# An adaLN feed-forward kernel on one core: K sums, a load of the down weights and three small steps are moved in the order of work

## The reference

```python
K = 2.0 * jnp.einsum('hn,hnl->hl', Cs, jnp.exp(P)).real     # 32 heads, n = 64, l = 512
y = causal_convolution(u * mask, K) + (u * mask) * D[:, None]
y = y * mask
```

```python
xq    = int4_quant(y)                          # beta = mean |y| of the row
gate  = bitlinear(xq, w_gate);  up = bitlinear(xq, w_up)      # 512 -> 1376
inter = int8_quant(up * square(relu(gate)))    # gamma = max |.| of the row
out   = x + bitlinear(inter, w_down)           # 1376 -> 512
```

## Time and profile before

| | |
|---|---|
| median of three runs | 205.91 us |
| the profiled execution's own time | 205.13 us |
| its span | 203.0 us |
| outside the span | 2.13 us |
| TensorE busy | 174.0 us (86%) |
| VectorE busy | 166.2 us (82%) |
| ScalarE (ACT) busy | 114.2 us (56%) |
| mean granted TensorE clock | 0.992 |

### The profile page before, as it was taken

The page is one execution under the profiler, slowest core; times in us unless marked ns, Lnnn a source line. Parts: engine busy times, 40 slices in busy tenths (PEclk is TensorE's granted clock), DMA queues, the critical chain, the costliest instruction groups (busy, mean ns, idle before and its releaser), DMA issues.

```text
span 203.0 us, 3423 instructions
## 1 busy us (share of the span) xinstructions
PE 174.0 (86%) x1127; PEld 93.7 (46%) x1143; DVE 166.2 (82%) x456; ACT 114.2 (56%) x188; POOL 11.7 (6%) x31
## 2 busy tenths in 40 slices
PE   1001699899899999999999999999999999998883
PEld 1001696554545454545454545454544454443352
DVE  6999888779997698888888878787878797978871
ACT  2186986799717282819191918182727364644730
POOL 8122500100001000000000000000000000000000
PEclk9999969999999999999999999999999999999999
DMA  2999939376898376756666665659565687245504
GB/s 84 371 385 338 316 103 332 124 247 124 164 187 174 138 152 204 151 164 143 176 133 185 134 182 135 184 129 183 132 182 149 157 137 181 67 96 56 116 6 103
DMA packets 48224, 34.12 MB, mean 168 GB/s; under 512 B 36512, under 2 KB 36880, under 8 KB 48208
## 3 DMA queue, kind: packets, MB, share of 16 engines
q1 hardware_dynamic: 47408, 32.38, 64.1%
q10 hardware_dynamic: 416, 1.47, 2.0%
q0 software_dynamic: 384, 0.06, 0.3%
HBM read 21.07 MB, written 4.28 MB: 125 GB/s over the span
## 4 chain that ended last, share of the span: by engine, by line
PE 70%; DVE 12%; DMA 7%; ACT 7%; issue 3%; SPq 0%; DVEq 0%; ACTq 0%
PE conv_ps L508 16%; PE gate_ps L591 15%; PE down_ps L641 15%; PE up_ps L596 14%; PE tr_act_ps L498 3%; DMA q_int<-y_i 2%; DMA toep<-k_back 2%; DMA k_back<-k_sb 2%; ACT g L749 1%; ACT int_gate L692 1%; ACT int_down L685 1%; DVE inter L1107 1%; PE tr_dve_ps L641 1%; PE up_ps L544 1%; PE tr_dve_ps L565 1%
## 5 line engine op out<-in xcount | busy, mean ns | idle before, releaser
L596 PE MATMUL up_ps<-up_t,q_t 128*128 128x416 bf16 (+2 forms) x192 | 45.0, 357 | 0.0
L707 ACT ACTIVATE y_abs<-y 128x512 bf16<-128x512 f32 x16 | 10.1, 629 | 61.1 <-DVE y L1022 61.1
L591 PE MATMUL gate_ps<-gate_t,q_t 128*128 128x416 bf16 (+2 forms) x177 | 41.9, 356 | 2.4 <-DVE q_t L1042 1.5
L1107 DVE SCALAR_TENSOR_TENSOR inter<-up_ps,gu_scale,g 128x416 f32<-128x416 f32 (+2 forms) x48 | 33.2, 692 | 6.8 <-issue 4.6
L508 PE MATMUL conv_ps<-toep,x_t 128*64 128x512 f32 (+3 forms) x256 | 38.0, 439 | 0.7 <-DMA toep<-k_back 0.5
L641 PE MATMUL down_ps<-down_t,i_t 128*128 128x512 bf16 (+1 forms) x153 | 35.3, 379 | 1.2 <-DVE i_t L1146 1.2
L749 ACT ACTIVATE g<-gate_ps,gu_scale 128x416 f32<-128x416 f32 (+2 forms) x48 | 30.3, 631 | 6.1 <-PE gate_ps L591 6.1
L1111 DVE TENSOR_REDUCE imax<-inter 128x1 f32<-128x416 f32 (+2 forms) x48 | 30.3, 631 | 1.6
L752 ACT ACTIVATE g<-g 128x416 f32<-128x416 f32 (+2 forms) x48 | 28.1, 585 | 1.5
L508 PEld LDWEIGHTS conv_ps<-toep,x_t 128*64 128x64 f32 x256 | 17.2, 136 | 23.5 <-issue 20.5
L596 PEld LDWEIGHTS up_ps<-up_t,q_t 128*128 128x128 bf16 x192 | 18.8, 98 | 18.4
(11 more groups left out here) (186 smaller groups left out, 170.9 us busy)
## 6 DMA issues: line engine op xcount, KB each, us to landing
toep<-k_back SPq DMA_DIRECT2D x16, 512.0 KB, 4.0
out_dram<-o_sb SPq DMA_DIRECT2D x30, 128.0 KB, 2.4
x_in<-in_x_dram SPq DMA_DIRECT2D x24, 128.0 KB, 3.1
raw_gate<-in_L_ffn_w_gate_dram SPq DMA_DIRECT2D x1, 1536.0 KB, 7.0
raw_up<-in_L_ffn_w_up_dram SPq DMA_DIRECT2D x1, 1536.0 KB, 13.5
raw_down<-in_L_ffn_w_down_dram ACTq DMA_DIRECT2D x1, 1376.0 KB, 6.9
raw_down<-in_L_ffn_w_down_dram SPq DMA_DIRECT2D x1, 1376.0 KB, 10.8
raw_gate<-in_L_ffn_w_gate_dram SPq DMA_DIRECT2D x1, 1024.0 KB, 9.3
```

The lines of the kernel that those rows point to most:

```text
L591: mm = pe.matmul(gate_ps[bank][:, 0:cn], q_t[p][:, i, :], gate_t[:, i, c0:c0 + cn], start=(i == 0), stop=(i == KB - 1))
L596: mm = pe.matmul(up_ps[bank][:, 0:cn], q_t[p][:, i, :], up_t[:, i, c0:c0 + cn], start=(i == 0), stop=(i == KB - 1))
L1107: v.scalar_tensor_tensor(out=inter[:, c0:c0 + cn], in0=up_ps[bank][:, 0:cn], scalar=gu_scale[p][:, 1:2], in1=g2[bank][:, 0:cn], op0=ALU.mu ...
```

## The change

Four things are moved; no arithmetic is changed.

1. SP no longer loads x of tile 1 in front of the zeros of `k_back`. After the Toeplitz tile of tile 0 it now loads x of tile 1, then half 0 of w_down, then the Toeplitz tile of tile 1, then half 1. The load of half 0 on ACT's queue is gone.
2. `k_sums(3)` leaves iteration 1. Its first four heads are multiplied in the prologue behind `k_sums(1)`, its last four behind `qt(0)`. `xt(0)` is put ahead of `mean(1)`.
3. On VectorE `q_copy(0)` is put ahead of `k_copy(2)`, and `q_copy(2)` ahead of the cast to i_t and of `gated(2)` in iteration 1.
4. On ACT `xt_copy(3)` is put ahead of `relu_square(2)` in iteration 1.

```diff
@@ sync
             load_x(0)
-            load_x(1)
...
+            def load_down(i):
+                s = weight_part(2, i)
+                sp.dma_start(raw[2][s], w_down.rearrange("(c p) i -> p c i", p=P)[s]).then_inc(w_loaded[2][i], 16)
+
             load_toep(0, 0)
+            load_x(1)
+            load_down(0)
             load_toep(1, 1)
-            s = weight_part(2, 1)
-            sp.dma_start(raw[2][s], w_down.rearrange("(c p) i -> p c i", p=P)[s]).then_inc(w_loaded[2][1], 16)
+            load_down(1)
             load_x(2)
@@ tensor
+        K_CUT = 3 * HG // 4
...
-            def k_sums(i):
+            def k_sums(i, first=0, last=HG):
...
-                for h in range(h0, h1):
+                for h in range(max(h0, first), min(h1, last)):
...
-                mm.then_inc(k_summed, 1)
+                if last >= h1:
+                    mm.then_inc(k_summed, 1)

             k_sums(0)
+            xt(0, 0, 0)
             mean(1)
-            xt(0, 0, 0)
             pe.wait_ge(tables_ready, 2)
             k_sums(1)
+            pe.wait_ge(winv_ready, 2)
+            k_sums(3, last=K_CUT)
             turn_inner(0, 0, range(3, IG))
...
             k_sums(2)
             qt(0)
+            k_sums(3, first=K_CUT)
...
-                if k == 1:
-                    k_sums(3)
@@ scalar
-            s = weight_part(2, 0)
-            act.dma_start(raw[2][s], w_down.rearrange("(c p) i -> p c i", p=P)[s]).then_inc(w_loaded[2][0], 16)
...
                 if k == 1:
                     y_round(2)
+                    xt_copy(3)
...
-                elif k < T - 2:
+                elif 2 <= k < T - 2:
                     xt_copy(m + 2)
@@ vector
             weight_copy(10)
+            q_copy(0, 0)
             k_copy(2)
-            q_copy(0, 0)
             down_sum(2)
...
                 if k in (1, T - 1):
                     gated(1)
+                if k == 1:
+                    q_copy(2, 0)
...
-                if 1 <= k < T - 1:
+                if 2 <= k < T - 1:
                     q_copy(m + 1, 1 - p)
```

## The result

| | median us | lowest to highest | runs |
|---|---|---|---|
| before | 206.11 | 205.87 to 206.24 | 5 |
| changed | 209.28 | 208.88 to 210.14 | 5 |

The ratio is 1.0152, with a 95% interval of 1.0117 to 1.0186: the change made the kernel slower, by 3.2 us. Here and in the experiments medians are of all runs, while ratios and their intervals leave out runs over 1.5% above the fastest of the same kernel (211.60 and 209.94 of e3, 208.15 of the kernel before). The profiled execution took 210.14, with a span of 208.2; it is the slowest of the five, and the kernel before was profiled in an execution of 205.13, under all five of its runs. So the rows show the loss larger (5.2 us by the spans, 208.2 against 203.0) than the medians do.

A forecast was written before the change was run, and what follows sets the result against it. Iterations run at TensorE's pace, so lateness before 60 us carries to the end; +2.4 - 0.2 - 0.7 + 1.3 = +2.8 on the profiled 205.13 gives 207.9, as a median 208.7; range 205.6 to 211.6.

The forecast's parts named there:

- A: The forecast case: stall at down_sum(0), two or three us net; 208.7 us, from 207.2 to 210.0; chance 0.55.
- Store and Toeplitz issue: Prologue: store of K's part 0 takes 2.2 us instead of 3.60; Toeplitz load issued at 26.1, 1.4 us gained.
- Landing of half 0: Prologue: half 0 of w_down lands at 34.9, so down_sum(0) starts then instead of at 32.49: +2.4 us.
- (b): Landing estimate for half 0 by parts: Toeplitz as measured, x and weights at 400 GB/s: 34.3.
- (c): Landing estimate for half 0 from half 1's measured load, stragglers included: 36.6.
- K sums: Prologue: half ahead of weight transposes hidden by the stall, up to 0.5 us without it; half behind qt(0) hidden.
- q_copy(0): VectorE ahead of the first products: q_copy(0) starts at once after qt(0), ahead of k_copy(2): -0.2 us.
- Iteration 1: Earlier xt_copy(3) starts conv(3) 1.03 us earlier, but down(1, 1) waits for down_copy(0): -0.7 us.
- TensorE's clock: TensorE stands from 37.1 to 39.6, then runs at half clock for 3.4 us: +1.3 us, bounds 0 and 1.7.
- C: Rival at down_sum(0): half 0 loads quickly, under 33.2, and the change wins; 205.2 to 205.5 us; chance 0.11.
- B: Rival at down_sum(0): half 0 lands later still, 36.6 to 38.0; 210.4 to 211.8 us; chance 0.15.
- E: Rival at conv(2): Toeplitz load of tile 2 late, about 1 us wait on top of A; 209.7 us; chance 0.12.

The follow-up runs named there:

- e3: The kernel before with only the new order of loads (x of tile 1 and half 0 behind the first Toeplitz load, half 0 on SP): 209.67 us, ratio 1.0134.
- e1: The changed kernel with half 0 of w_down back on ACT's queue at its old place: 205.55 us, ratio 0.9975 to the kernel before.
- e7: The changed kernel with half 0 of w_down still on SP's queue, but issued right behind x of tile 0: 204.70 us, ratio 0.9932 to the kernel before.
- e4: The changed kernel with nine unread filler matmuls between k_sums(2) and qt(0): 207.85 us, ratio 1.0109 to the kernel before.
- e6: The kernel before with only k_sums(3) moved as in the change and xt(0) ahead of mean(1): 205.99 us, ratio 1.0012.
- e9: e7 with xt_copy(3) and q_copy(2) of iteration 1 back at their old places: 205.53 us, ratio 0.9983 to the kernel before.
- e2: The changed kernel with down_sum(0) moved on VectorE from ahead of y_mask(0) to behind k_copy(2): 206.97 us, ratio 1.0067 to the kernel before.
- e5: e1 with the first four heads of k_sums(3) just ahead of conv(0) instead of the weight transposes: 205.32 us, ratio 0.9966 to the kernel before.
- e8: e7 with the first four heads of k_sums(3) just ahead of conv(0) instead of the weight transposes: 205.37 us, ratio 0.9951 to the kernel before.

## Why the prediction held, point by point

The forecast was 208.7, the measured median 209.28, and the case was A, the stall at down_sum(0). e1 and e7 show the cause: with the load early, on either queue, the wait and the loss are gone.

**Store and Toeplitz issue.** 2.2 us and 26.1 were said; 2.23 us and 26.41 measured (k_copy(0) itself was 0.25 later). The store did gain by the free DMA engines, and e1, with half 0 beside it again (a store of 4.15 us), issued its Toeplitz load at 28.37. The same store took 1.61 us in e4 and 2.67 in e3, so 2.2 is the middle of a range.

**Landing of half 0.** 34.9 was said, 35.85 came: 7.85 us after its issue. It lies between bounds (b) and (c), 34.3 and 36.6, nearer to (c) than I took it. e3 and e4 have the same wait, until 36.1 and 35.5. y_mask(0) came 3.35 later than in the profiled kernel before instead of 2.4: 0.95 more, and that is the landing.

**K sums.** Ahead of the transposes they were hidden behind the stall, as said, and without that cover the 0.5 us named for it did not show in the median of e6, whose interval could hide it; in its trace y_mask(0) was 0.58 late. Behind qt(0) they are hidden only at full clock (e4: 0.64 us). At half clock they took 1.03 and held the products 0.4 us: a price that the prediction had at nothing. It put the fall of the clock at about 40.1, behind qt(0), and it came at about 39.6, ahead of it. But even its own figures held the price: the fall stood 0.4 ahead of the products, and the K sums were said to take 1.0 at half clock.

**q_copy(0).** It started at once behind qt(0); the 0.2 us were there in e4, and in the changed kernel were eaten by the K sums.

**Iteration 1.** -0.7 was said, 0.6 found in the trace, with down(1, 1) waiting for down_copy(0) as named. e7 against e9 gives 0.34 by the start of down(1, 1) and 0.5 to 0.7 by their runs.

**TensorE's clock.** The fall was foreseen, and its size was too small: 3.4 us at half clock and 1.3 us of loss were said; the profiled execution had some 6.8 us of it and lost 2.1 at the products and conv(1) and 0.3 ahead of them. TensorE was also busier before the fall than was thought, 1.68 of 3.4 us instead of under 1.0. But this term isn't fixed. In e3 the same stall went by at full clock; e4 puts what it is worth in the median at 1.2 to 1.4 us, with intervals that overlap. That the clock falls because of the stall is supported by e1 (no stall, no fall) and e2 (a fall behind the wait one tile on); e3 shows that it need not.

**Why the median was met better than the trace.** The sum for the profiled execution was +2.8 against +5.2, the one for the median +2.8 against 3.2 to 3.4 (209.28 against 206.11 or 205.91). The two measured losses differ by where the profiled executions lie: the kernel before's is 1.0 under its median, the changed kernel's 0.9 above its own. It did not simply have the longest fall: the mean granted clocks of the five runs are 0.984 (the profiled one), 0.983, 0.990, 0.989 and 0.984, and the one at 0.983 took 208.88. The two errors of size, the landing (0.95) and the clock (1.1), went to the same side, so a miss of 0.6 in the median is in part luck. A likely offset, estimated and not shown: most runs of the kernel before begin y_mask(0) about 1 us later than its profiled one did (35.2 in e1, e5 and e8 against 34.09), and the wait for the load swallows that lateness, while the prediction added the full stall to their median. What the other four executions of the changed kernel lost to the clock isn't known; only one was profiled.

**The rivals.** C, the quick load, is refuted by L = 35.85 against its 33.2. B's later landing, 36.6 and more, was approached, not reached. In E the Toeplitz load of tile 2 makes conv(2) wait; it was issued at 44.50, and conv(2), at 52.26, did not wait.

What stays open is why the runs of e3 differ by 5 us. Both the clock and something else have a part: two runs with a mean granted clock of 1.000 took 206.62 and 208.58, 2 us apart, and the other four, at 0.976 to 0.992, took 209.63 to 211.60. Whether that something is the landing of the load isn't shown; only one run was profiled.

## What to carry to other kernels

A load may be moved only as far as the first instruction that reads it, and that is often not the work it is meant for: here a sum that is needed by a matmul nearly 10 us later stands in an in-order list just ahead of the instruction that everything waits for. Before moving a DMA, look in that engine's list for its first reader and how much slack it has; if it has none, move the reader too, and then check what that reader now stands ahead of (e2). With the same load early in the same queue (e7), the rest of the change made the kernel 0.7% faster than before.

## What the runs showed of the hardware

The granted clock can be lost behind a stretch in which TensorE still works half of the time: it was busy 1.68 of 3.4 us before the two stretches at 0.50 and 0.59. It is not certain either: 1.79 of 3.4 in e3 was followed by full clock. Nor is half idle needed: in e7 a stretch at 0.70 (26.5 to 29.9 us) followed one in which TensorE was busy 2.82 of 3.5. So these rows give no rule by the share of busy time. With nine matmuls without use in such a gap (e4) the median was 1.2 to 1.4 us lower, with intervals that overlap.

The row of the granted clock can't be taken for the pace of TensorE in the prologue: the changed kernel's is 1.00 from 26.5 to 29.9 us while twelve transposes took 1.38 us, as long as at a granted 0.50 before. Executions of the kernel before with a dip on record were faster (median 205.46) than those without (206.09).

A load of 1376 KB took 7.85 us from issue to landing behind 768 KB in the same queue. A store of 8 KB took 1.61 to 2.67 us with nearly nothing else moving (e4 1.61, changed 2.23, e3 2.67) and 3.60 to 4.15 beside that load (before 3.60, e6 3.78, e1 4.15): a small store ahead of a dependent load was late by the large transfer under way.
